# Routed expert groups with merged instructions, expert scales read in place, and gamma applied ahead of the scatter

## The reference

```python
x = _layernorm(x + causal_attention(x))        # q, k of width 16, values are x itself
x = _layernorm(x + x @ ternary(weight).T)      # 256x256
x = _layernorm(x + L1_attn(x))                 # statistics of q, k over channels, a small
                                               # convolution net per batch of 512, gate on v, proj
x = _layernorm(x + L1_ffn(x))
```

```python
h = (x - mu) / jnp.sqrt(var + LN_EPS) * ln_gamma + ln_beta
sw1, sw2 = _bit_quant(shared_w1), _bit_quant(shared_w2)      # (512,256), (256,512)
shared_out = silu(h @ sw1.T) @ sw2.T
probs = softmax(h @ router_w.T); top_prob = max(probs); top_idx = argmax(probs)   # 8 experts
ew1, ew2 = _bit_quant(expert_w1), _bit_quant(expert_w2)      # row-wise ternary times a scale
h1 = silu(einsum('btd,efd->ebtf', h, ew1)); eo = einsum('ebtf,edf->ebtd', h1, ew2)
routed_out = einsum('ebtd,bte->btd', eo, one_hot(top_idx) * top_prob)
return shared_out + routed_out
```

## Time and profile before

| | us |
|---|---|
| three timed runs | 911.54, 917.33, 918.01 (median 917.33) |
| profiled execution, its own time | 912.14 |
| its span, first to last instruction | 910.8 |
| start until the first projection on PE | 22.6 |
| first group's rows copied out by ACT | 689.8 |
| last group's rows copied out by ACT | 884.2 |

### The profile page before, as it was taken

The page is one execution under the profiler, slowest core; times in us unless marked ns, Lnnn a source line. Parts: engine busy times, 40 slices in busy tenths (PEclk is TensorE's granted clock), DMA queues, the critical chain, the costliest instruction groups (busy, mean ns, idle before and its releaser), DMA issues. The chain is left out here.

```text
span 910.8 us, 18608 instructions
## 1 busy us (share of the span) xinstructions
PE 782.4 (86%) x5514; PEld 621.8 (68%) x5514; DVE 727.4 (80%) x2321; ACT 698.1 (77%) x1561; POOL 315.1 (35%) x384
## 2 busy tenths in 40 slices
PE   0568899999999999999999999988757878888783
PEld 0346678778878878878878877866435767767672
DVE  1777999778878878888887887977563889989995
ACT  0447887688697697697697797786746989999995
POOL 2000001012422323323333323434561555556556
PEclk9976999999999999999999999999887999999997
DMA  7132331110221211201203201101127775445441
GB/s 201 60 116 92 124 122 57 47 49 24 82 67 40 76 54 52 82 19 65 83 18 111 82 20 41 37 30 48 47 83 218 181 203 164 151 146 167 130 106 56
DMA packets 50979, 80.81 MB, mean 89 GB/s; under 512 B 8954, under 2 KB 27838, under 8 KB 50880
## 3 DMA queue, kind: packets, MB, share of 16 engines
q1 hardware_dynamic: 39056, 53.46, 20.7%
q0 software_dynamic: 9984, 25.29, 7.7%
q10 hardware_dynamic: 1840, 0.86, 0.3%
HBM read 49.57 MB, written 32.11 MB: 90 GB/s over the span
## 5 line engine op out<-in xcount | busy, mean ns | idle before, releaser
L3621 POOL DMA_INDIRECT out<-G_y,Gid x80 | 83.1, 1039 | 77.8 <-ACT G_y L1867 56.1
L1220 PE MATMUL bank<-E2T,G_Sh 128*128 (+1 forms) x320 | 74.3, 278 | 39.7 <-DVE G_Sl L3426 39.6
L3493 POOL DMA_INDIRECT rrec<-R,pos x64 | 64.3, 1005 | 82.0 <-DVE R L2111 67.2
L1849 ACT ACTIVATE G_S<-bank,e1b,e1s 128x256 f32<-128x256 f32 x160 | 91.6, 693 | 0.0
L519 PE MATMUL bank<-X,PT 128*128 128x257 f32 x320 | 82.5, 392 | 2.5 <-DVE X L1954 1.3
L3484 POOL DMA_INDIRECT hrec<-HN,pos x64 | 65.3, 1020 | 52.0 <-DVE pos L2234 37.2
L3452 POOL TENSOR_TENSOR R<-rstd,mhalf 128x4 f32<-128x4 f32 x16 | 17.4, 1089 | 184.2 <-DVE rstd L1910 184.2
L1208 PE MATMUL bank<-G_T,E1T 128*128 128x256 f16 x640 | 80.0, 280 | 1.0 <-DVE G_T L3417 1.0
L3460 POOL TENSOR_TENSOR R<-V,mhalf 128x8 f32<-128x8 f32 x16 | 26.7, 1666 | 142.7 <-DVE V L1920 142.7
L1220 PE MATMUL bank<-E2T,G_Sl 128*128 (+1 forms) x320 | 74.6, 278 | 0.0
L1208 PEld LDWEIGHTS bank<-G_T,E1T 128*128 (+1 forms) x640 | 64.4, 101 | 9.7 <-issue 1.4
(11 more groups left out here) (362 smaller groups left out, 2597.5 us busy)
## 6 DMA issues: line engine op xcount, KB each, us to landing
G_r<-rrec SPq DMA_DIRECT2D x40, 258.0 KB
G_h<-hrec SPq DMA_DIRECT2D x40, 257.0 KB, 2.8
X<-in_x SPq DMA_DIRECT2D x16, 512.0 KB, 5.2
XT<-in_xT SPq DMA_DIRECT2D x16, 512.0 KB, 4.3
e1n<-in_ew SPq DMA_DIRECT2D x8, 512.0 KB, 3.4
e2n<-in_ew SPq DMA_DIRECT2D x8, 512.0 KB, 3.4
rrec<-rpad SPq DMA_DIRECT2D x18, 129.0 KB, 4.9
hrec<-hpad SPq DMA_DIRECT2D x18, 128.5 KB, 4.7
```

The costliest lines, as they stand in the source:

```text
L1220: last = pe.matmul(banks[j][:, 0:D], x[w % NGB][:, f, j * P:(j + 1) * P], E2T[:, expert_of[w], f, :], start=k == 0, stop=k == 2 * FC - 1)
L1849: act.activation(G_S[w % 2][:, ff, :], bk[:, (ff - f0) * SLOT:(ff - f0 + 1) * SLOT], ACT.Silu, bias=e1b[:, expert_of[w], ff], scale=e1s[:, ...
L3493: pool.indirect_dma_start(rrec[:], bass.IndirectOffsetOnAxis(pos[b % 2][:, j:j + 1], 0), R[b % 2][:, j, :], None).then_inc(s[f"rrec{b % 2} ...
L3621: pool.indirect_dma_start(t["out"], bass.IndirectOffsetOnAxis(Gid[w % 6][:, j:j + 1], 0), G_y[w % 3][:, j, :], None, bounds_check=TOK - 1, ...
```

## The change

1. The splits of a group become single instructions: `gT`, `gTl`, `gSh` and `gSl` one each over the double width. The semaphore counts follow.
2. `ge2` is gone. `gy` reads the scales where they lie, in `e2s`, at an address from a register; DVE reads the expert's number itself, and ACT's reading moves to `gsilu`.
3. Gamma is multiplied in once, in the front: `rest` gets a step that makes `gamx` (NREST is 51), and POOL's new `hg(b)` multiplies the batch's `HN` by it after PE has transposed it and before the scatter. `gT` and `gTl` lose their gamma operand.
4. Since `HN[0]` is no longer reused in the groups, it stays as it is. `gid_` gets a new wait: group w-6 must have landed in the output.
5. The order lists of all five engines are written anew: start, front, and the group loops.

```diff
-            for c in range(DC):
-                act.activation(G_T[w % NGB][:, 0, c, :], banks[6 + w % 2][:, c * SLOT:(c + 1) * SLOT], ACT.Copy,
-                               scale=gamc[:, c:c + 1]).then_inc(s["gT"], 1)
+            act.activation(G_T[w % NGB][:, 0].rearrange("p c n -> p (c n)"), banks[6 + w % 2][:], ACT.Copy).then_inc(s["gT"], 1)
...
-            act.activation(G_Sh[w % NGB][:, f0:f0 + 2], G_S[w % 2][:, f0:f0 + 2], ACT.Copy, scale=sdn[:]).then_inc(s["gSh"], 1)
+            act.activation(G_Sh[w % NGB][:], G_S[w % 2][:], ACT.Copy, scale=sdn[:]).then_inc(s["gSh"], 1)
...
-        for w in range(48):
-            gsilu(w - 4, 0)
-            gT(w - 2)
-            gn(w - 7, 0)
-            gSh(w - 4, 0)
-            gsilu(w - 4, 1)
-            ge2(w - 3)
-            gn(w - 7, 1)
-            gSh(w - 4, 1)
+        for w in range(47):
+            gsilu(w - 3, 1)
+            gT(w - 1)
+            gn(w - 6, 0)
+            gn(w - 6, 1)
+            gSh(w - 3)
+            gsilu(w - 2, 0)
```

On DVE (its group loop), with `gTl` a `tensor_tensor` of 512 columns and `gSl` one instruction of 1024:

```diff
+                    expert_of[w] = bass.DynSlice(dve.value_load(q_exi[0:1, w:w + 1], min_val=0, max_val=NE - 1), 1)
...
-        for w in range(48):
-            gTl(w - 3)
+        for w in range(47):
+            gy(w - 6, 0)
             gve(w - 7)
-            gSl(w - 5, 0)
-            gy(w - 6, 0)
+            gSl(w - 5)
             gy(w - 6, 1)
             gnb_(w - 7)
             gx(w - 6, 0)
-            gSl(w - 5, 1)
             gx(w - 6, 1)
             gbn(w - 6, 0)
             gbn(w - 6, 1)
             gmv(w - 6, 0)
+            gTl(w - 2)
             gmv(w - 6, 1)
```

On POOL:

```diff
+        def hg(b):
...
+            pool.wait_ge(s["hT"], at("hT", b, 1))
+            h = HN[b % 2][:, :, 0:D]
+            pool.tensor_tensor(h, h, gamx[:, None, :].to_broadcast([P, NT, D]), ALU.mult).then_inc(s["hg"], 1)
...
             pool.wait_ge(s[f"gath{w % NGR}"], 16 * (w // NGR + 1))
+            if w >= 6:
+                pool.wait_ge(s[f"out{w % 3}"], 16 * NGT * ((w - 6) // 3 + 1))
             pool.tensor_copy(Gid[w % 6][:], G_h[w % NGR][:, :, D].bitcast(I32)).then_inc(s["gid"], 1)
...
-        for w in range(48):
-            gid_(w - 2)
+        for w in range(47):
+            scatter(w - 6, 1)
             gpower(w - 5)
-            scatter(w - 6, 1)
             scatter(w - 5, 0)
+            gid_(w)
```

On SP, in the groups and at the start:

```diff
-            rload(w - 8)
-            gload(w - 3)
-            pads(w - 4)
+            rload(w - 7)
+            gload(w - 1)
+            pads(w - 7)
...
-        for i in range(3):
-            load_small(i)
+        load_small(0)
+        load_xT(0)
+        load_expert(0)
+        load_x(0)
+        load_small(1)
+        load_x(1)
+        load_small(2)
         pad_rows()
+        load_expert(1)
+        load_xT(1)
```

More of the change, by code:

```diff
@@ new lines, in act_program @@
+        exp(3, 3)
+        oexp2(0)
+        map_E1(8)
+        for i in range(4):
+            x2s(2, i)
+        map_s(8)
+        sq3(0, 0)
+        sq3(0, 1)
+        TTh_(2, 0)
+        sq3(0, 2)
+        sq3(0, 3)
+        TTh_(2, 1)
+        x1c(3, 0)
+        for i in range(4):
+            hn(0, i)
+        sq3(1, 0)
+        x1c(3, 1)
+        gate_r(2)
+        HT_(0, 0)
+        x1c(3, 2)
+        x1c(3, 3)
+        HT_(0, 1)
+        for g in range(2, 8):
+            sq3(2 * g - 3, 1)
+            gexp(2 * g - 2)
+            T1h_(2 * g - 1, 0)
+            sq3(2 * g - 3, 2)
+            sq3(2 * g - 3, 3)
+            PS_(2 * g - 2)
+            silu(2 * g - 4, 0)
+            Sh_(2 * g - 4, 0)
+            T1h_(2 * g - 1, 1)
+            silu(2 * g - 4, 1)
+            Sh_(2 * g - 4, 1)
+            silu(2 * g - 4, 2)
+            Mh_(2 * g - 2)
+            Sh_(2 * g - 4, 2)
+            map_r0(5 * g)
+            silu(2 * g - 4, 3)
+            Sh_(2 * g - 4, 3)
+            qk(2 * g)
+            sq2(2 * g - 1, 0)
+            sq2(2 * g - 1, 1)
+            rexp(2 * g - 4)
@@ new lines, in act_program @@
+            hn(2 * g - 3, 2)
+            U_(2 * g - 2, 0)
+            map_r1(5 * g)
+            hn(2 * g - 3, 3)
+            for i in range(3):
+                x2s(2 * g - 1, i)
+            U_(2 * g - 2, 1)
+            HT_(2 * g - 3, 0)
+            HT_(2 * g - 3, 1)
+            map_s(5 * g - 1)
+            x2s(2 * g - 1, 3)
+            nmr_(2 * g)
+            U_(2 * g - 2, 2)
+            TTh_(2 * g - 1, 0)
+            silu(2 * g - 3, 0)
+            map_E0(5 * g)
+            TTh_(2 * g - 1, 1)
@@ L1798, in act_program @@
         Sh_(14, 3)
-        sq3(15, 2)
-        sq3(15, 3)
+        for i in range(4):
+            sq3(15, i)
         rexp(14)
@@ L3258, in dve_program @@
+        chw(15, 0)
+        x2p(14, 3)
+        router(13, 3)
+        Sl_(13, 0)
+        qks(15, 1)
+        chw(15, 1)
+        x2p(15, 0)
+        place(12, 0)
+        qks(15, 2)
+        router(13, 4)
+        chw(15, 2)
+        place(12, 1)
+        qks(15, 3)
+        ode(7, 0)
+        router(13, 5)
+        ode(7, 1)
+        ode(7, 2)
+        chw(15, 3)
+        place(12, 2)
+        for i in range(3, 6):
             ode(7, i)
         place(13, 0)
+        ode(7, 6)
+        ode(7, 7)
@@ L3260, in dve_program @@
         x2p(15, 1)
-        chw(15, 3)
-        r(12, 2)
-        acc(13)
-        ode(7, 8)
-        ode(7, 9)
-        Sl_(13, 0)
-        rs3(13)
-        rg(12)
-        for i in range(10, 13):
-            ode(7, i)
-        x2p(15, 2)
-        ode(7, 13)
-        Sl_(13, 1)
+        Sl_(13, 1)
+        for i in range(8, 11):
+            ode(7, i)
+        place(13, 1)
+        for i in range(11, 14):
+            ode(7, i)
+        Sl_(13, 2)
+        Sl_(13, 3)
+        ode(7, 14)
+        ode(7, 15)
@@ L3274, in dve_program @@
+        place(13, 2)
+        for i in range(16, 19):
+            ode(7, i)
+        rs3(13)
+        ode(7, 19)
         Ml_(15)
-        for i in range(14, 20):
-            ode(7, i)
-        r(12, 3)
-        Sl_(13, 2)
+        y(13, 0)
         ode(7, 20)
         ode(7, 21)
-        router(13, 6)
-        for i in range(22, 25):
+        x2p(15, 2)
+        ode(7, 22)
+        ode(7, 23)
+        y(13, 1)
+        for i in range(24, 27):
             ode(7, i)
-        Sl_(13, 3)
-        ode(7, 25)
@@ L3365, in dve_program @@
         r(15, 3)
+        for i in range(4, 10):
+            sort(i)
+        expert_of = {}
         def gy(w, j):
```

2233 lines of the change are left out of this document (1071 added, 1162 removed).

## The result

The changed kernel takes 992.48 us in the median of four runs (989.52 to 995.85), before 914.74: a ratio of 1.085, 95% interval 1.079 to 1.091. The forecast was 902 with a range up to 916, so sign and range both missed. The profiled execution took 995.85 us, its span is 994.4. The first `gT` starts at 740.1 us instead of 689.8, and from there to the end are 254.3 us instead of 221.0. So 50 us are lost ahead of the groups and 33 in them.

The account below looks back on a forecast made before the run. PE was taken to bound the front and ACT the groups, there replaced by POOL's closed loop after the change. 912.1 - 6 (groups) - 7.5 (start) + 0.5 (gamma) = 899, forecast put 3 above at 902 us, range 886 to 916.

Parts of the forecast that it names:

- Gamma on POOL: Front: sixteen hg of 2 to 3 us each, free while POOL is idle; 0.5 us charged, bounds 0 and 4.6.
- My sum has 0 for it: Front: what hg could do to DVE, called open, was entered in the sum as 0.
- The second rival: Front: POOL's product blocks DVE 16 times, up to 2 us each; chance 0.16 of an end above 912.
- Order of the front: Front: PE is full at 79.93 of 80 us, so a new order saves only at start and handover.
- Groups, forecast -6 us: Group stage: -11.6 for shorter intervals, -0.3 for the first five, +1.5 for the drain, +4.5 net for padding.
- ACT's work: Groups: falls from 5.03 to 4.36 us per group, bounds 4.31 and 4.41.
- The closed loop through POOL: Groups: from gn to gn through two scatters, copy and power, 4.69 us (4.55 to 4.95), longer than ACT's 4.36.
- DVE loses two fixed parts: Groups: DVE saves some 0.1 us for each of two fixed parts.
- Padding and the new wait: Groups: gid_ waits for group w-6 to land; 1.2 us extra for each of eight groups, 9.5, bounds 0 and 17.
- Start, -7.5 us: Start: reordered loads bring rest(8) from 32.99 to about 25 us; 7.5 us earlier, bounds 3 and 10.
- ACT stays the bound: Rival, groups: POOL's steps overlap more, a group takes 4.36 us, 11 us less, end at 891; chance 0.17.
- `gy`'s register read: Groups: DVE's register reading in front of gy, taken as 0; if exposed, at most half a us in 32 groups.

Follow-up runs that it names:

- after_again: The changed kernel without any edit, measured again on the chip of row_before, split_nohg and best: 961.51 us, ratio 1.057.
- row_before: The kernel before with POOL's scatters of one front turn put in a row, seven behind gnr: 910.08 us, ratio 1.000.
- best: The kernel before with the change's start (SP's and DVE's) and with ge2 gone, scales read in place: 892.34 us, ratio 0.981.
- split_nohg: gsl_split without POOL's product hg, the rows without gamma: 921.99 us, ratio 1.012.
- gsl_split: The changed kernel with gSl again as two instructions of 512 columns at the same place: 940.69 us, ratio 1.033.
- power_first: The changed kernel with the next group's power ahead of the second scatter in POOL's group loop: 991.51 us, ratio 1.086.
- gsl_later: The changed kernel with DVE's merged gSl moved behind gnb_: 960.17 us, ratio 1.053.
- spread: The changed kernel with POOL's row of eight scatters in each front turn broken up, hg kept: 968.67 us, ratio 1.064.
- both_front: The changed kernel without hg (rows without gamma) and with the row of eight scatters broken up: 954.72 us, ratio 1.046.

## Why the prediction was wrong, point by point

The plainest sum is from after_again, which has no late results: its span is 47.9 us over that of before, 17.8 until the first `gT` and 30.1 behind it. The first measurement had 83.6; of the difference, 32.5 us lie ahead of the first `gT`. Four kernels on one chip split the 18 us ahead of the groups: the first `gT` goes from 689.6 (row_before) to 679.3 with the new start (best), to 688.1 with the new order of the front (split_nohg), and to 707.6 with `hg` (after_again).

- **Gamma on POOL, charged 0.5 us: the first step that failed.** It costs 16.8 us until the first `gT` (gsl_split less split_nohg) or 19.5 (after_again less split_nohg), 2.7 to 3 in each turn. The product's own time, 2.20 us in the mean, was well estimated. The failed step is "My sum has 0 for it", the effect on DVE. It rested on a POOL power over eight columns, which says nothing about one of 1024. The second rival had place and mechanism right, but not its chance. It also added up wrongly: from 902, a loss of 1.6 us for each of sixteen ends at 928 and one of 2 us at 934, not at 915 and 921. The Trainium skill (SBUF — State Buffer, SBUF: two separate sides) says that of a DVE instruction with two SBUF inputs and a POOL instruction that reads SBUF, the one that starts first gets a shared port pair for its whole length and "the other fully blocks". The trace agrees on the blocking: 3.47 instead of 0.74 us beside a long POOL product. On who goes first it agrees in the groups, but not in the front, where the record of `Sl` begins 0.73 us ahead of `hg` and `hg` still goes first.
- **Order of the front, counted as neutral.** "None of PE's instructions there changes, so a new order can save only where PE is not full" was applied to gains alone. Without `hg` and late results a turn takes 72.4 us against 69.65. On one chip the order costs 8.8 us until the first `gT` (best to split_nohg); taken as what is left of the 17.8 without the start (-11.8) and `hg` (16.8) it is 12.8.
- **Groups, forecast -6 us, were +30 to +33.** ACT's work did fall as forecast; four silu, `gT`, both `gn` and `gSh` take 1.79, 0.48, 0.99 and 1.04 us from start to start, 4.3 in sum. The closed loop through POOL was named and bounds as said. Its sum of 4.69 held the second scatter at 0.97; it takes 1.95 behind the start of the merged `gSl`, and these 0.98 us are nearly all of the 1.08 by which the interval (5.77) was over the forecast; times 34 they are 33 of the 36 us by which the groups were off, the largest miss of all. This is the mis-sized term, and it was the price of an edit that I booked as a gain ("DVE loses two fixed parts"). Undone alone it brings 18.6 us (251.1 to 232.5 us of groups). With two short `gSl` the loop is still 5.24, since one of them still begins ahead of the scatter and holds it to 1.42 (or, where the scatter is first, the power to 1.18). So the new POOL order would have lost against 5.03 even then.
- **Padding and the new wait.** Right in kind, too high in size: of the nine intervals while padding was written, four took 6.6 to 7.7 us and five 5.0 to 5.9, in sum 4.7 us over nine steady ones, where 9.5 were forecast. POOL's copy did wait for the landing in some of them, up to 1.5 us.
- **Start, -7.5 us, was -10.3 to -11.8.** Right in kind; `rest(8)` came at 22.22, not 25.
- **ACT stays the bound** was wrong, as said, and `gy`'s register read left at most 0.35 us of idle time in some groups.
- **Late results** stood in no rival. They cost the first measurement some 30 us, and I cannot say what they are. In the turns they were seen only with POOL's order of the changed kernel, never with that of before; the changed kernel had them in the first measurement and not in after_again. It is not the chip alone: power_first and gsl_later have the same front and ran on one chip, with turns of 79.7 and 76.9 us and waits of up to 4.8 and 1.0 us on late results within them. They stayed when `hg` was taken out. That the row of eight scatters makes them is not shown: gsl_split has that row and none of them, and spread and both_front, which break it up, still show some behind the last turn. Whether a chip that has them would show them with row_before was not tried.

## What to carry to other kernels

Merging instructions is not free when another engine shares something with this one: an instruction that begins first can hold the other engine to its end, so ask what a 1.3 us instruction meets and which of the two begins first, not only what fixed cost it saves. Cutting an instruction in two shortens the hold only if the other engine gets in between. When work is moved to an idle engine, price it by what it holds up beside it and who waits for that, and when a step is moved into a closed loop, write the loop out with the duration that each step has next to its new neighbours. And take a large change apart: here two of its parts gained 18 us together while the rest lost 70 to 96.
